# Local attention: keys laid out by token through DMA, and a mask product over part of each span

## The reference

```python
def _L2_attn_ref(x, Wq, Wk, Wv, Wu, bu):
    EMB, HEADS, K = (64, 8, 32)
    ...
    xp = jnp.pad(x, ((0, 0), (k - 1, 0), (0, 0)))
    q = (x @ Wq.T).reshape(b, t, h, e) / scale
    kk = (xp @ Wk.T).reshape(b, tp, h, e) / scale
    v = (xp @ Wv.T).reshape(b, tp, h, e)
    idx = jnp.arange(t)[:, None] + jnp.arange(k)[None, :]
    kw = kk[:, idx]
    vw = v[:, idx]
    dot = jnp.einsum('bthe,btkhe->bthk', q, kw)
    attn = jax.nn.softmax(dot, axis=-1)
    out = jnp.einsum('bthk,btkhe->bthe', attn, vw)
    out = out.reshape(b, t, h * e)
    return out @ Wu.T + bu
```

## Time and profile before

| | |
|---|---|
| Median of 3 runs | 1396.29 us (1394.86 to 1397.76) |
| The profiled execution | 1398.01 us, its span 1396.2 us |
| Mean granted TensorE clock | 0.956 |
| Busy in the span: PE, PEld | 1282.8 us, 792.0 us |
| Busy in the span: DVE, ACT, POOL | 606.6 us, 639.1 us, 190.3 us |
| DMA | 26.92 MB in 39032 packets |

### The profile page before, as it was taken

The page is one execution under the profiler, slowest core; times in us unless marked ns, Lnnn a source line. Parts: engine busy times, 40 slices in busy tenths (PEclk is TensorE's granted clock), DMA queues, the critical chain, the costliest instruction groups (busy, mean ns, idle before and its releaser), DMA issues. The chain is left out here.

```text
span 1396.2 us, 28368 instructions
## 1 busy us (share of the span) xinstructions
PE 1282.8 (92%) x12234; PEld 792.0 (57%) x12234; DVE 606.6 (43%) x1008; ACT 639.1 (46%) x1217; POOL 190.3 (14%) x206
## 2 busy tenths in 40 slices
PE   8999989888888799999789999999999999978766
PEld 5223338777777688888734444444444444466554
DVE  3992114111112577777523333334333333366643
ACT  2996744324577445454523433343343333432430
POOL 4100014940000422222040001000100000002000
PEclk9988999999999799999889999999999999999977
DMA  5900000000002300000400000000000000050002
GB/s 112 124 1 1 1 1 5 1 0 1 1 1 77 106 4 4 4 4 4 109 14 1 1 0 1 1 1 1 0 1 1 1 1 0 1 122 1 0 1 61
DMA packets 39032, 26.92 MB, mean 19 GB/s; under 512 B 25181, under 2 KB 37533, under 8 KB 38909
## 3 DMA queue, kind: packets, MB, share of 16 engines
q1 hardware_dynamic: 38525, 24.05, 8.1%
q10 hardware_dynamic: 384, 1.07, 0.3%
HBM read 22.90 MB, written 2.21 MB: 18 GB/s over the span
## 5 line engine op out<-in xcount | busy, mean ns | idle before, releaser
L1272 DVE TENSOR_TENSOR sp_sums<-sp_y,sp_shared 64x512 f32<-64x512 f32 (+1 forms) x256 | 176.3, 689 | 288.0 <-PE sp_y L1145 283.8
L1145 PE MATMUL sp_y<-hankel,sp_ut 128*128 128x512 f16 x1152 | 276.9, 381 | 1.4 <-DVE sp_ut L1255 1.4
L1243 ACT COPY sp_sums<-sp_y 64x512 f32<-64x512 f32 x256 | 148.6, 580 | 263.6 <-PE sp_y L1145 254.6
L1145 PEld LDWEIGHTS sp_y<-hankel,sp_ut 128*128 128x128 f16 x1152 | 111.4, 98 | 150.1 <-issue 22.5
L1205 PE MATMUL sp_o<-sp_sums,mix 128*64 128x128 f32 (+2 forms) x1024 | 122.8, 390 | 0.0
L1145 PE MATMUL sp_y<-hankel_sum,sp_ut 128*128 128x512 f16 x384 | 104.0, 380 | 0.0
L503 PE MATMUL convv<-runningv,toeplitz 128*128 128x128 f32 x610 | 83.7, 283 | 12.7 <-DVE runningv L523 12.7
L503 PE MATMUL convh<-runningh,toeplitz 128*128 128x128 f32 x610 | 84.0, 283 | 8.1 <-DVE runningh L523 8.1
L1205 PEld LDWEIGHTS sp_o<-sp_sums,mix 128*64 128x64 f32 x1024 | 64.0, 134 | 44.1 <-issue 33.5
L503 PEld LDWEIGHTS convv<-runningv,toeplitz 128*128 128x128 f32 x610 | 74.1, 191 | 20.7 <-DVE runningv L523 20.1
L503 PEld LDWEIGHTS convh<-runningh,toeplitz 128*128 128x128 f32 x610 | 72.9, 189 | 14.5 <-DVE runningh L523 14.2
(11 more groups left out here) (329 smaller groups left out, 2033.7 us busy)
## 6 DMA issues: line engine op xcount, KB each, us to landing
hankel<-phi_rows SPq DMA_DIRECT2D x32, 192.0 KB, 4.5
hankel_sum<-phi_rows SPq DMA_DIRECT2D x32, 128.0 KB, 3.3
ex_w<-in_L_ffn_weight SPq DMA_DIRECT2D x1, 2080.0 KB
m_plus<-in_L_ffn_M_phi_plus SPq DMA_DIRECT2D x2, 1024.0 KB, 13.9
m_minus<-in_L_ffn_M_phi_minus SPq DMA_DIRECT2D x2, 1024.0 KB, 16.5
out<-x SPq DMA_DIRECT2D x8, 256.0 KB, 3.3
x<-in_x ACTq DMA_DIRECT2D x2, 512.0 KB, 7.9
x<-in_x SPq DMA_DIRECT2D x2, 512.0 KB, 9.3
```

The lines of the kernel that those rows point to most:

```text
L1145: mm = nc.tensor.matmul(out[:, :, :], ut[g % 2][:, hu, b, s, :, :].rearrange("p a c -> p (a c)"), table[:, hf, 2 * j:2 * j + 2, lo:lo + SPAN],
L1243: nc.scalar.copy(sums[HALF[a], :, b, to], y_ps[r][HALF[a], :, of]).then_inc(y_c[r], 1)
L1272: nc.vector.tensor_tensor(sums[HALF[a], :, b, to], y_ps[r][HALF[a], :, of], shared[done % 2][HALF[a], :, of], op).then_inc(y_c[r], 1)
```

## The change

`layernorm_stage` gets an optional place for its token-major scaled piece. For the norm ahead of the attention this is a slice of `m.normed`, so that all 32 chunks stay there token-major; VectorE's wait for the turned-back piece is left out in this case. `windows_turned`, its copy on ScalarE and their semaphores go. In their place SP fills `xt`, now one of three, from `m.normed` by six DMAs per chunk: for each of the four windows of 112 tokens the tokens of this chunk, and for the first two windows also the last 32 or 16 tokens of the chunk before, or zeros at a pair's start (`before`, cleared by GpSimd). SP waits for the value products of chunk i - 3 before it issues chunk i's, and `attend(i)` waits for all six. The mask product is written over the first and the last 16 columns of each span of 48 only, 256 columns in place of 384; the 16 between, where the mask is zero, are first written by the scores.

```diff
@@ -633,7 +633,7 @@
-def layernorm_stage(nc, m, out_piece, tag, extra=None):
+def layernorm_stage(nc, m, out_piece, tag, extra=None, by_token=None):
@@ -648,11 +648,14 @@
         sb, pb, sem = open_pools(nc, ctx)
         square = [sb(f"square{tag}{k}", [P, 2 * TP, C]) for k in range(2)]
         var, dev, inv = (sb(f"{n}{tag}", [P, N, 2 * TP]) for n in ("var", "dev", "inv"))
-        scaled = [sb(f"scaled{tag}{k}", [P, 2 * TP, C]) for k in range(2)]
+        scaled = [sb(f"scaled{tag}{k}", [P, 2 * TP, C]) for k in range(2)] if by_token is None else None
...
+        def scaled_piece(u):
+            return scaled[u % 2][:, :, :] if by_token is None else by_token(u)
         with nc.Block() as block:
             @block.tensor
             def _(pe):
...
-                        mm = nc.tensor.transpose(back[u % 2][:, j * P:(j + 1) * P], scaled[u % 2][:, 2 * j:2 * j + 2, :].rearrange("p a c -> p (a c)"), m.ident[:, :])
+                        mm = nc.tensor.transpose(back[u % 2][:, j * P:(j + 1) * P], scaled_piece(u)[:, 2 * j:2 * j + 2, :].rearrange("p a c -> p (a c)"), m.ident[:, :])
                     mm.then_inc(back_ok, 1)
             @block.scalar
...
-                        if u > 2:
+                        if u > 2 and by_token is None:
                             dve.wait_ge(back_ok, u - 2)
-                        nc.vector.tensor_tensor(scaled[(u - 1) % 2][:, :, :], centred[(u - 1) % (AHEAD + 1)][:, :, :],
+                        nc.vector.tensor_tensor(scaled_piece(u - 1), centred[(u - 1) % (AHEAD + 1)][:, :, :],
                                                 inv[:, u - 1, :].to_broadcast([P, 2 * TP, C]), ALU.mult).then_inc(scaled_ok, 1)
...
-    layernorm_stage(nc, m, piece, "w", history)
+    def by_token(u):
+        return m.normed[:, u * PER_UNIT:(u + 1) * PER_UNIT, :].rearrange("p n (a c) -> p (n a) c", c=C)
+    layernorm_stage(nc, m, piece, "w", history, by_token)
...
+    RING = 3
...
-        xt = [sb(f"win_xt{k}", [P, 4, P]) for k in range(2)]
+        xt = [sb(f"win_xt{k}", [P, 4, P]) for k in range(RING)]
+        before = sb("win_before", [WINDOW, P])
...
-        xt_ps, o_ps = q_ps[:, 0, :, :], z_ps[:, 0, 0, 0:2, :, :].rearrange("p j h n -> p (j h n)")
+        o_ps = z_ps[:, 0, 0, 0:2, :, :].rearrange("p j h n -> p (j h n)")
...
+        xt_in = [sem(f"w_xt_in{k}") for k in range(RING)]
+        MOVES = 6
...
+        def corners(row):
+            return row.rearrange("p (v t k) -> p v t k", t=KEYS // SUB, k=SUB)[:, :, 0::2, :]
         with nc.Block() as block:
+            @block.sync
+            def _(sp):
+                sp.wait_ge(cleared, 1)
+                for i in range(CHUNKS):
+                    if i >= RING:
+                        sp.wait_ge(z_ok, i - RING + 1)
+                    for t in range(4):
+                        old = max(WINDOW - t * SUB, 0)
+                        if old:
+                            src = m.normed[CHUNK - old:CHUNK, i - 1, :] if i % PER_PAIR else before[0:old, :]
+                            sp.dma_start(xt[i % RING][0:old, t, :], src).then_inc(xt_in[i % RING], 16)
+                        first = t * SUB + old - WINDOW
+                        sp.dma_start(xt[i % RING][old:LONG, t, :], m.normed[first:first + LONG - old, i, :]).then_inc(xt_in[i % RING], 16)
             @block.gpsimd
             def _(pool):
+                nc.gpsimd.memset(before[:, :], 0.0).then_inc(cleared, 1)
                 nc.gpsimd.memset(probs[:, :, KEYS:C], 0.0).then_inc(padded, 1)
                 for i in range(CHUNKS):
                     if i == 1:
@@ -823,20 +853,10 @@
                     if i:
                         pe.wait_ge(q_dve, i)
                         pe.wait_ge(q_act, i)
-                    if i > 1:
-                        pe.wait_ge(xt_c, i - 1)
...
-                def windows_turned(i):
-                    pe.wait_ge(q_act, min(i + 2, CHUNKS))
-                    if i:
-                        pe.wait_ge(xt_c, i)
-                    for t in range(4):
-                        mm = nc.tensor.transpose(xt_ps[0:LONG, t, :], m.pieces[:, i, t * SUB:t * SUB + LONG], m.ident[:, :])
-                    mm.then_inc(xt_ok, 1)
...
-                        nc.tensor.matmul(s_ps[:, r, 0:NW * KEYS], m.win_rows[:, :], m.win_mask[:, :], start=True, stop=True)
+                        nc.tensor.matmul(corners(s_ps[:, r, 0:NW * KEYS]), m.win_rows[:, :], corners(m.win_mask[:, :]), start=True, stop=True, skip_group_check=True)
...
-                def attend(i, odd):
+                def attend(i):
                     pe.wait_ge(pt_act, i + 1)
                     pe.wait_ge(pt_dve, i + 1)
-                    pe.wait_ge(xt_c, i + 1)
+                    pe.wait_ge(xt_in[i % RING], 16 * MOVES * (i // RING + 1))
                     if i:
                         pe.wait_ge(o_c, i)
                     for p in range(2):
@@ -890,11 +910,11 @@
                             for high in range(2):
                                 rows = slice(high * C, high * C + KEYS)
                                 for r in range(2):
-                                    mm = nc.tensor.matmul(z_ps[HALF[r], high, p, t, :, :].rearrange("p h n -> p (h n)"), xt[odd][rows, t, p * C:(p + 1) * C],
+                                    mm = nc.tensor.matmul(z_ps[HALF[r], high, p, t, :, :].rearrange("p h n -> p (h n)"), xt[i % RING][rows, t, p * C:(p + 1) * C],
                                                           probs_t[rows, r, p, t // 2, (t % 2) * C:(t % 2 + 1) * C], start=True, stop=True)
                     mm.then_inc(z_ok, 1)
...
-                    attend(i, odd)
-                    if loops(i, 1):
-                        windows_turned(i + 1)
+                    attend(i)
...
-                def take_windows(i, odd):
-                    act.wait_ge(xt_ok, i + 1)
-                    if i > 1:
-                        act.wait_ge(z_ok, i - 1)
-                    nc.scalar.activation(xt[odd][0:LONG, :, :], xt_ps[0:LONG, :, :], ACT.Copy).then_inc(xt_c, 1)
-
...
-                    if loops(i, 1):
-                        take_windows(i + 1, 1 - odd)
                 take_queries(0)
                 exps(0)
                 take_queries(1)
-                take_windows(0, 0)
...
```

More of the change, by code:

```diff
@@ L792, in window_attention_stage @@
         z_ps = pb("z_ps", [P, 2, 2, 4, HP, SUB])
-        xt_ps, o_ps = q_ps[:, 0, :, :], z_ps[:, 0, 0, 0:2, :, :].rearrange("p j h n -> p (j h n)")
+        o_ps = z_ps[:, 0, 0, 0:2, :, :].rearrange("p j h n -> p (j h n)")
         scored = s_ps[:, :, 0:NW * KEYS].rearrange("p r (v n) -> p r v n", n=KEYS)
-        (padded, q_ok, q_act, q_dve, s_ok, xt_ok, xt_c, sub_ok, p_ok, pt_ok, pt_act, pt_dve, z_ok, max_ok, sum_ok, inv_ok, n_ok,
+        (padded, q_ok, q_act, q_dve, s_ok, cleared, sub_ok, p_ok, pt_ok, pt_act, pt_dve, z_ok, max_ok, sum_ok, inv_ok, n_ok,
          zt_c, o_ok, o_c) = (sem("w_" + n) for n in (
-             "padded", "queries", "queries_act", "queries_dve", "scores", "xt", "xt_taken", "shifted", "probs", "probs_turned", "pt_act", "pt_dve",
+             "padded", "queries", "queries_act", "queries_dve", "scores", "before_cleared", "shifted", "probs", "probs_turned", "pt_act", "pt_dve",
              "heads", "max", "sum", "inv", "normed", "heads_taken", "out", "added"))
+        xt_in = [sem(f"w_xt_in{k}") for k in range(RING)]
+        MOVES = 6
         def image(p, half):
@@ L892, in attend, with body @@
                                 for r in range(2):
-                                    mm = nc.tensor.matmul(z_ps[HALF[r], high, p, t, :, :].rearrange("p h n -> p (h n)"), xt[odd][rows, t, p * C:(p + 1) * C],
+                                    mm = nc.tensor.matmul(z_ps[HALF[r], high, p, t, :, :].rearrange("p h n -> p (h n)"), xt[i % RING][rows, t, p * C:(p + 1) * C],
                                                           probs_t[rows, r, p, t // 2, (t % 2) * C:(t % 2 + 1) * C], start=True, stop=True)
                     mm.then_inc(z_ok, 1)
-                def body(i, odd):
+                def body(i):
                     if loops(i, 1):
@@ L911, in _ @@
                 query(1)
-                windows_turned(0)
                 for i in range(CHUNKS):
-                    body(i, i % 2)
+                    body(i)
                 output(LAST)
```

## The result

| | before | after |
|---|---|---|
| median of 13 runs, us (lowest to highest) | 1394.86 (1389.13 to 1403.86) | 1388.27 (1381.26 to 1394.58) |
| profiled execution, us (its span) | 1398.01 (1396.2) | 1381.26 (1379.5) |
| 28 steady chunks of the attention, us | 178.6 | 171.1 |

The ratio is 0.9947, 95% interval 0.9926 to 0.9968: 6.6 us faster by the medians, where 18.3 were forecast. 1388.27 lies outside the forecast range. The profiled execution is the fastest of its 13, so the 16.7 us between the two spans overstate the gain; of them the attention stage holds some 11.2 (its 28 steady chunks 7.5, its start and end the rest), and the other 5.5 lie in other stages, most of which the change does not touch.

What follows compares the result with a forecast made beforehand. TensorE's instruction stream was taken to bound the attention, at 6.31 us per chunk, then a loop at 5.71: 30 x 0.60 = 18.0, plus 0.3 for early masks, 18.3 us; 1396.29 - 18.3 = 1378.0, range 1374.5 to 1384.0.

Steps and rivals of the forecast that it cites:

- The turns, 0.58: Local attention, TensorE: removing the window turns before the mask saves 0.58 us per chunk, bounds 0.41 and 0.58.
- Rival (a): Attention, TensorE: the gap moves behind the value products and the mask's saving is lost; 12.3 us gained, 1384.0, chance 0.15.
- The mask, 0.107: Attention, TensorE: two mask matmuls of 256 columns for 384 save 0.107 us per chunk, bounds 0 and 0.107.
- What is late next: Attention: a loop through TensorE, VectorE and GpSimd becomes the bound, at 5.69 us per chunk, 5.71 with a second wake.
- its sign, the wait of L891: Attention: TensorE waits briefly on GpSimd before each chunk's turns of the probabilities, under 0.1 us, showing the loop has taken over.
- The moves at no cost: Attention: six SBUF-to-SBUF DMAs per chunk cost nothing; issue 3.5 or 4.4 us, under 5.7; other engines not slowed.
- rival (c): Attention: the moves come one after another, a chunk takes 14.4 us, 243 us more, 1639; chance 0.04.
- The step that failed: Attention: TensorE, busy all 20 us of the steady stretch, sets the time; what leaves its stream is worth its full length.

Runs made afterwards that it cites:

- turns_only: The changed kernel with the full mask product of the kernel before; median 1390.83 us, ratio 0.9963.
- mask_only: The kernel before with only the shorter mask product of the change; median 1391.97 us, ratio 0.9984.
- the two experiments: no_moves, and the kernel before with six moves per chunk into tiles that nobody reads, the latter 1393.10 us, ratio 0.9987.
- after_again: The changed kernel, unaltered, profiled and timed once more; median 1389.44 us, ratio 0.9946 to the kernel before.
- no_moves: The changed kernel with the DMA moves of the first three chunks alone, output wrong; median 1388.25 us, ratio 0.9942.
- half_attend: The changed kernel with value products of two windows in one matmul, 281 instructions per chunk for 345, output wrong; 1374.20 us, ratio 0.9857.

## Why the prediction was wrong in its size

- **The turns, 0.58.** Right: the base fell by 6.31 - 5.68 = 0.63 with both edits, by 6.31 - 5.73 = 0.58 in turns_only. Rival (a), a gap that stays, fell.
- **The mask, 0.107.** Right as a step (pair 0.39 for 0.49; base 6.31 to 6.21). What it is worth in the sum by itself is not settled: none in mask_only's profile, 0.16% in its times.
- **What is late next.** Right: the loop through VectorE and GpSimd, 5.68 against 5.71, with its sign, the wait of L891.
- **The moves at no cost.** Right: no wait on a DMA, share 0.16 (forecast 0.2 to 0.3), VectorE and ScalarE at their old durations, and the two experiments. This is the rest of the stage's DMA view (KB each, median us to landing) and SP's issues of one chunk:

```profile
win_xt<-normed SPq DMA_DIRECT2D x64, 56.0 KB, 2.0
win_xt<-normed SPq DMA_DIRECT2D x32, 48.0 KB, 1.9
win_xt<-normed SPq DMA_DIRECT2D x32, 40.0 KB, 2.3
```

```profile
552.51 0.53 SPq L833 DMA_DIRECT2D win_xt<-normed  x1
553.09 0.88 SPq L835 DMA_DIRECT2D win_xt<-normed  x1
554.01 0.59 SPq L833 DMA_DIRECT2D win_xt<-normed  x1
554.64 1.87 SPq L835 DMA_DIRECT2D win_xt<-normed  x3
```

Six issues take 3.9 us, where 3.5 to 4.4 were the bounds; rival (c) fell.

- **The step that failed** is the first: "So TensorE's instruction stream sets the time, and what leaves it is worth its full length, until some chain through other engines takes over." It took the stream for work in the array alone, and the loops through other engines for the only thing that could take over. The stream has a second bound, the supply of instructions: a block of 256 is not entered before 1.2 us after its load has landed. The earlier trace rows was close to it already: 354 instructions in 6.31 us are 17.8 ns each. The change took much time out of the array and only 9 of 354 instructions out of the stream. At 18.0 ns, 345 want 6.21 us, and 28 of them 173.9; the three profiles of this stream (after, after_again, no_moves) gave 171.1, 175.9 and 170.7, a mean of 172.6, against the forecast 28 x 5.71 = 159.9. From before's 178.6 that is a gain of 6.0, and the medians differ by 6.6. With the supply relieved (half_attend) the forecast's sum was met.

No rival named this. What could have: the irregular "issue" gaps inside one kind of matmul that the kernel before already had (three long periods of 28), and a stage in which TensorE's instructions are short and many. That the time fell, as forecast, is no luck: the array's time did shorten, and the supply left a third of the gain.

The Trainium skill, "Runtime: NRT & Kernel Launch", section "Instruction fetch mechanics", says that instructions come in blocks of 16 KiB, 256 at a time. The trace agrees, with 16 KB per load and 252 recorded instructions for each. It also says that the fetch is hidden, because the sequencer's own floor of about 20 cycles an instruction is slower than the refill. Here stops of over a microsecond end 1.2 to 1.6 us after a load, each at the boundary of a block, so it is not hidden in this stage.

**Left open.** The stops are waits for a refill and not the sequencer's own pace, since they lie at the boundaries of the blocks alone. What sets the time of a refill is open. A load takes 0.9 to 1.6 us, and its instructions run 1.2 us after it at the earliest. But it starts anywhere from 1.0 us before TensorE enters the block ahead of it to 3.5 us after (over all 14 traces), and what starts it no trace here shows. So 18 ns is an average of this stage and no rate of its own: two loads of the kernel before began only 3.26 us apart (532.43 and 535.70), which is 12.7 ns an instruction.

## What to carry to other kernels

Count the instructions of the busiest engine per loop step and divide the step's time by them, before costing an edit. In this stage TensorE stood at about 18 ns (weight loads, matmuls and waits together); from there, time taken out of the array brought a third of its worth (6.6 us of 18.3), and fewer, wider matmuls brought the rest (half_attend, whose output is wrong). Whether 18 ns holds for another mixture of instructions no run here shows; what to look for are idle times that lie a multiple of 256 instructions apart. A bound by supply does not look like a wait: the base step gets shorter as planned and some steps get longer, so read the sum over many steps and not the one step that is well to see. Moving an operand by DMA from a tile that exists already can be free, as here at six issues of 0.6 us per 5.7 us step on an idle queue.

## What was not expected of the hardware

- The average of TensorE's instructions in this stage never got under 17.7 ns where the supply was the bound (170.7 us / 28 / 345), though within the scores pairs of weight load and matmul start some 15 ns apart for a while (64 of them from 565.46 to 566.39): instructions that have been loaded run faster than loads come, and then TensorE stops at the end of the block.
- Of 70 stops in 12 traces every one lies at the boundary of a block of 256 instructions and ends 1.2 to 1.6 us after the load of the next block has landed.
- The granted clock can fall to 0.50 for 3.4 us behind such a stop, in the middle of a stage in which TensorE is busy for over 90% of the time: five times in three traces.
- Moves within SBUF of 40 to 56 KB landed in 1.9 to 2.3 us, and at a DMA share of 0.16 they did not lengthen TensorE's stops (no_moves has the same eight) or the operations of VectorE and ScalarE that the prediction names.
